# Layer 0 of a two-layer kernel: masks stacked under key parts, three fp16 products in place of f32, another order of work on every engine

## The reference

```python
x = L0_attn_x
xn = layernorm(x)
q, k, v = split(xn @ w_qkv.T)                 # 32, 8 and 8 heads of 64
q, k = rope(rms_norm(q, q_norm_w)), rope(rms_norm(k, k_norm_w))
scores = q @ k.T / 8 + mask                   # -inf outside causal window of 64
attn = softmax(scores) @ v
x = x + attn @ w_out.T + down(silu(gate(xn)) * up(xn))
xn = layernorm(x)
x = x + L1_attn(xn) + L1_ffn(xn)              # L1_attn: LN with ln_w, ln_b; qkv = Xn @ W_in; ...
```

## Time and profile before

| | us |
|---|---|
| median of three runs | 1190.95 |
| the runs | 1176.71 to 1191.04 |
| the profiled execution | 1181.03 |
| its span, first to last instruction | 1179.2 |

### The profile page before, as it was taken

How to read it: one execution, slowest core, us unless ns; L and a number is a source line. 1 busy time by engine, 2 the same in 40 slices (tenths; PEclk the granted TensorE clock), 3 DMA queues, 4 the chain that set the end, 5 groups by cost and what they waited for, 6 DMA issues and landing times. The chain is left out here.

```text
span 1179.2 us, 26751 instructions
## 1 busy us (share of the span) xinstructions
PE 1124.7 (95%) x8985; PEld 676.9 (57%) x8985; DVE 764.1 (65%) x1624; ACT 703.0 (60%) x1703; POOL 709.7 (60%) x1003
## 2 busy tenths in 40 slices
PE   4999999999999999999999999678999999999997
PEld 2677777777777777777777776454333333333324
DVE  5865555656556556556556555447999989887841
ACT  2545445544545445545445444226999999888992
POOL 4777777777777777778778767332455554242221
PEclk9999999999999999999999999879999999999998
DMA  7010100001000000100000000050000000000001
GB/s 277 16 55 22 28 11 21 24 12 26 18 17 22 23 16 21 23 16 22 23 15 22 12 15 18 10 160 1 2 2 3 2 2 2 11 11 11 11 2 36
DMA packets 45801, 30.65 MB, mean 26 GB/s; under 512 B 27684, under 2 KB 44004, under 8 KB 45156
## 3 DMA queue, kind: packets, MB, share of 16 engines
q1 hardware_dynamic: 45668, 28.95, 8.8%
HBM read 18.49 MB, written 4.19 MB: 19 GB/s over the span
## 5 line engine op out<-in xcount | busy, mean ns | idle before, releaser
L1208 DVE TENSOR_REDUCE l_mxv<-l_mx 128x1 f32<-128x1024 f32 x256 | 300.2, 1219 | 39.7 <-PE l_mx L1392 37.2
L1111 ACT ACTIVATE l_prob<-l_sc 128x512 f32<-128x512 f32 x512 | 270.7, 610 | 13.1 <-PE l_sc L1400 12.7
L442 ACT ACTIVATE probs<-sc,neg_bound 128x512 f32<-128x512 f32 x128 | 88.0, 687 | 259.5 <-PE sc L848 259.5
L525 DVE TENSOR_TENSOR t<-qk,tcw 128x320 f32<-128x320 f32 x128 | 62.9, 491 | 248.0 <-ACT v L354 247.1
L649 POOL TENSOR_TENSOR t<-t 128x320 f32<-128x320 f32 x128 | 110.4, 862 | 175.9 <-DVE t L526 175.8
L1392 PE MATMUL l_mx<-l_kt,l_qt 48*128 48x512 f16 x512 | 154.0, 382 | 9.4 <-DVE l_mxv L1208 9.4
L1400 PE MATMUL l_sc<-l_qt,l_kt 50*128 50x512 f16 x512 | 159.4, 382 | 0.9 <-ACT l_prob L1111 0.8
L1372 PE MATMUL l_acc<-l_prob,qkv_all 128*17 128x256 f32 x2048 | 153.9, 384 | 0.0
L640 POOL TENSOR_TENSOR rm<-ss,half_neg 128x5 f32<-128x5 f32 x128 | 152.6, 1192 | 0.0
L807 PE MATMUL pv<-v,probs 128*128 128x65 f32 x1024 | 141.4, 281 | 0.0
L834 PE MATMUL ob<-wo,ats 128*128 128x256 f32 x512 | 131.9, 380 | 0.5 <-ACT ats L354 0.5
(11 more groups left out here) (180 smaller groups left out, 2307.9 us busy)
## 6 DMA issues: line engine op xcount, KB each, us to landing
v<-v SPq DMA_DIRECT2D x240, 16.2 KB, 1.8
qkv_all<-w_qkv SPq DMA_DIRECT2D x3, 768.0 KB, 8.5
xn_all<-xs SPq DMA_DIRECT2D x16, 128.5 KB, 2.0
xa<-x SPq DMA_DIRECT2D x16, 128.0 KB, 2.5
wo<-w_o SPq DMA_DIRECT2D x2, 1024.0 KB, 8.6
xc<-x SPq DMA_DIRECT2D x16, 128.0 KB, 2.3
out<-xc SPq DMA_DIRECT2D x16, 128.0 KB, 2.0
l_wt<-w SPq DMA_DIRECT2D x2, 1024.0 KB, 8.2
```

What stands on the lines that cost most here:

```text
L1111: act.activation(prob[:, (y * NI + u) % NPR, h * 512:(h + 1) * 512], sc[:, k % NSC, :], ACT.Exp, scale=D1 ** -0.5).then_inc(s_["act_sc"], 1)
L1208: dve.tensor_reduce(mxv[:, x % 2, u:u + 1], mx[:, MX[k] % 2, :], AX.X, ALU.max).then_inc(s_["dve_mx"], 1)
```

## The change

**Scores.** The key high part is stored on both halves of the partitions, for a product of full height with `qt` (query low over query high). The low part of the keys stands in the lower half (partitions 64 to 127) of two further stretches of `kts`, with the mask in the upper half, and is multiplied with `qe`, which holds an identity over the query high part. Mask and low part are one product of full height for each window. ScalarE fills in the masks once, in slots 4 and 5. The first two tiles add one more mask product. The second half of S and its wait are gone. The key is turned in two full pieces instead of four half ones.

**Three fp16 products.** `wo` and `win` are loaded into `stage` (four pieces and one, SP waiting for the splits of wq that free the place) and split into high and low fp16 parts, in slots 8 to 15 and 20, 22, 24, on ScalarE and VectorE. The turned context is split too: high part on ScalarE (`ath`), low part on VectorE (`atl`). W is then six fp16 products and the layer-1 projections six each. v is scaled by 8 and the residual sum divides by 512.

**ln_w and ln_b** are applied by ScalarE, as scale and bias of the copy after the turn (Identity); a further copy and a VectorE subtraction split the result. GpSimd's two products are gone.

**Order.** TensorE: gate and up first, A, O, the down projection (a step of its own), V, T, S, W. ScalarE: Tanh and the context's high part ahead of the squares, exp ahead of the key copies. VectorE: context's low part first; sums of squares after the division; query copies last, after the normalisations and the ranking. GpSimd: the table products one a slot over four slots, the rotation over three. The layer-1 projection begins in slot 3 instead of 4 of its tile, and takes one slot more.

```diff
-    return (n + 2) * G + 7 if n >= NT - 2 else (n + 3) * G + 4
+    return (n + 2) * G + 21 - n if n >= NT - 2 else (n + 3) * G + 3
...
+def gated(s):
+    i, r = divmod(s - LAG_F0 - (s < LAG_F0 + 2 * G), 2 * G)
+    return (i, r // 2) if 0 <= i < NI and r % 2 == 0 and r // 2 < NF else (None, None)
...
             # SP
-                if s in (LAG_A + 1, LAG_A + 3):
-                    j = (s - LAG_A) // 2
-                    sp.dma_start(wo[:, j * 4:j * 4 + 4, :, :], w_o[:, j * 4:j * 4 + 4, :, :]).then_inc(wo_ld[j], 16)
+                if s in (LAG_A + 1, LAG_A + 4):
+                    j = 0 if s == LAG_A + 1 else 1
+                    sp.wait_ge(s_["dve_wq"], 6 if j else 3)
+                    for c in range(2 * j, 2 * j + 2):
+                        sp.dma_start(wo_f[c], w_o[:, 2 * c:2 * c + 2, :, :]).then_inc(wo_ld[j], 16)
...
                 if s == 2 * G:
+                    sp.wait_ge(s_["dve_wq"], G)
-                    sp.dma_start(win[:, :, :], w_in).then_inc(l1w_ld, 16)
+                    sp.dma_start(win_f, w_in).then_inc(l1w_ld, 16)
...
             # ScalarE
+                k = s - LAG_W + 1
+                if 0 <= k < G:
+                    act.wait_ge(wo_ld[k // 4], 16 * 2)
+                    ev(wo_hi[:, k, :, :], wo_f[k // 2][:, k % 2, :, :], WS).then_inc(s_["act_w1"], 1)
...
-                    ev(xt1[:, :, :], extra[:, 0:D].rearrange("p (k t) -> p k t", k=KC)).then_inc(s_["act_xat"], 1)
+                    for c in range(KC):
+                        ins = act.activation(xlt[:, c, :], extra[:, c * P:(c + 1) * P], ACT.Identity,
+                                             bias=lnb[:, c:c + 1], scale=lnw[:, c:c + 1])
+                    ins.then_inc(s_["act_xat"], 1)
+                    act.wait_ge(s_["act_xat"], n * 2 + 1)
+                    ev(xt1h[:, :, :], xlt).then_inc(s_["act_xat"], 1)
...
-                    ev(nat[:, b, :, 0:HD], t1[:, b, :, :]).then_inc(s_["act_hi"], 1)
+                    ev(nat[:, b, 0:REP * P].rearrange("p (h d) -> p h d", h=REP)[:, :, HD:P], t1[:, b, 0:REP, :])
+                    ev(nat[:, b, REP * P + HD:NH * P + HD].rearrange("p (a d) -> p a d", a=2),
+                       t1[:, b, REP:NH, :].broadcast_to([P, 2, HD])).then_inc(s_["act_hi"], 1)
...
-                    ev(kts[:, n % B, :, k, 0:WIN], kts[:, n % B, :, k, P:P + WIN]).then_inc(s_["act_kc"], 1)
+                    ev(kts[:, n % B, k, 0:WIN], kts[:, n % B, k, P:P + WIN])
+                    ev(kts[under, n % B, k, near:near + WIN], kts[under, n % B, k, far + WIN:far + P]).then_inc(s_["act_kc"], 1)
+                if s in (LAG_A, LAG_A + 1):
+                    o = far if s > LAG_A else near
+                    act.wait_ge(mk_ld, 16)
+                    ev(kts[upper, :, :, o:o + P].rearrange("p b g c -> p (b g) c"),
+                       mk[upper, 1:2, :].broadcast_to([HD, B * G, P]))
...
-                    ev(kts[:, n % B, :, k, WIN:WIN + P], tr[:, REP:REP + 2, :]).then_inc(s_["act_kt"], 1)
+                    ev(kts[:, n % B, k, WIN:WIN + P], tr[:, REP, :])
+                    ev(kts[under, n % B, k, near + WIN:4 * P].rearrange("p (a c) -> p a c", a=2),
+                       tr[under, REP + 1:REP + 2, :].broadcast_to([HD, 2, P])).then_inc(s_["act_kt"], 1)
...
             # VectorE
+                n, k, ok = at(s, LAG_O)
+                if ok:
+                    dve.wait_ge(s_["act_at"], n * G + k + 1)
+                    wait(dve, s_["pe_W"], n * G + k - 1)
+                    dve.tensor_tensor(atl[:, b, :, :, :].rearrange("p a h q -> p h a q"), atv,
+                                      ath[:, b, :, :, :].rearrange("p a h q -> p h a q"), ALU.subtract).then_inc(s_["dve_al"], 1)
...
+                n = on_way(s, 1)
+                if n is not None:
+                    dve.wait_ge(s_["act_xat"], n * 2 + 2)
+                    dve.tensor_tensor(xt1l[:, :, :], xlt, xt1h[:, :, :], ALU.subtract).then_inc(s_["dve_xt"], 1)
...
+                n, k, ok = at(s, LAG_T)          # now the last block of the loop
+                if ok:
+                    dve.wait_ge(s_["act_kt"], n * G + k + 1)
+                    wait(dve, s_["pe_S"], n * G + k - 1)
+                    dve.tensor_copy(qt[:, b, :, :], tr[:, 0:REP, :])
+                    dve.tensor_copy(qe[under, b, :, :], tr[under, 0:REP, :]).then_inc(s_["dve_qt"], 1)
...
             # TensorE
+                    for j in range(REP + 2):
+                        o = j * P if j < REP else REP * P + HD if j == REP else REP * P - HD
+                        ins = pe.transpose(tr[:, j, :], nat[:, b, o:o + P], idh[:, :])
...
-                        pe.wait_ge(s_["act_at"], t * G + j + 1)
+                        pe.wait_ge(s_["dve_al"], t * G + j + 1)
...
-                    pe.matmul(weights[0], keys(n, k, 1, 0, top), queries(k, 0, top), start=True, stop=False)
-                    pe.matmul(weights[1], outside(n, 1), eyes, start=True, stop=False)
-                    pe.matmul(weights[0], keys(n, k, 0, 0, full), queries(k, 0, full), start=False, stop=False)
-                    pe.matmul(weights[1], keys(n, k, 0, 1, full), queries(k, 1, full), start=False, stop=False
-                              ).then_inc(s_["pe_S1"], 1)
+                    for h in range(2):
+                        ins = pe.matmul(weights[h], fine(n, k, h), queries(qe, k, h), start=True, stop=False)
+                    if n < B:
+                        pe.matmul(weights[0], mk[upper, 0, :], eyes, start=False, stop=False)
+                    for h in range(2):
+                        ins = pe.matmul(weights[h], coarse(n, k, h), queries(qt, k, h), start=False, stop=True)
...
-                        ins = pe.matmul(ob[:, 0:D], ats[:, b, j, :, :], wo[:, k, j, :], start=(k == 0 and j == 0),
-                                        stop=False)
+                        for m, (a, w) in enumerate(((ath, wo_hi), (ath, wo_lo), (atl, wo_hi))):
+                            ins = pe.matmul(ob[:, 0:D], a[:, b, j, :, :], w[:, k, j, :], start=(k == 0 and j == 0 and m == 0),
+                                            stop=(k == G - 1 and j == 1 and m == 2))
...
+                    terms = [(c, a, w) for c in range(KC) for a, w in ((xt1h, win_hi), (xt1h, win_lo), (xt1l, win_hi))]
+                    for m, (c, a, w) in enumerate(terms):
+                        ins = pe.matmul(extra[:, :], a[:, c, :], w[:, c, 0:2 * D], start=(m == 0), stop=(m == len(terms) - 1))
```

More of the change, by code:

```diff
@@ L32 @@
 RMS_EPS, LN_EPS = 1e-6, 1e-5
-WS = 64.0
+WS, VS = 64.0, 8.0
 HID = 704
@@ L594, in _ @@
                     norm_stats(st3, mv3, ve3, xs[:, par, 0:D], par, "dve_b3", "dve_g3", "dve_v3", n)
-                    wait(dve, s_["dve_h"], min(NI * NF, max(0, (s - LAG_F0) // 16 * NF + min(NF, (s - LAG_F0) % 16 // 2 + 1))))
+                    wait(dve, s_["dve_h"], sum(gated(r)[0] is not None for r in range(s + 1)))
                     if n == 0:
@@ L708, in _ @@
[L708 to L712 removed]
+                for r in range(3):
+                    n = on_way(s, 4 if s >= (NT + 1) * G + 2 else 4 + r)
+                    if n is None:
+                        continue
                     heads = qk1_all[:, n % B, n // B, :].rearrange("p (h d) -> p h d", d=D1)[:, :, 0:ROT1]
@@ L854, in _ @@
                     wait(pe, s_["dve_xl"], n)
-                    wait(pe, s_["act_l1"], sum(way(j) + 2 < s for j in range(NT)) * 2)
+                    wait(pe, s_["act_l1"], sum(way(j) + 3 < s for j in range(NT)) * 2)
                     for c in range(KC):
```

345 lines of the change are left out of this document (180 added, 165 removed).

## The result

The changed kernel takes 1105.28 us, median of four runs from 1092.86 to 1113.09; the kernel before, beside it, 1190.99. The ratio is 0.927, interval 0.915 to 0.939: faster. The forecast was 1110 in a range of 1094 to 1142. The profiled execution took 1092.86 us, span 1091.1.

A forecast was written before the change was run, and what follows sets the result against it. TensorE's own work was taken to set layer 0's pace. Span 1179.2 - 89.6 (TensorE) + 10 (waits) + 6 (start) - 1.5 (end) = 1104.1, time 1106, taken as 1110; range 1094 to 1142.

The forecast's parts named there:

- Output projection: TensorE, each slot: six fp16 products at 0.65 us instead of 0.96; gain 0.31 x 128 slots = 39.7 us.
- Scores: TensorE, each slot: four full products, 0.44 us instead of 0.67, a half-height pair counted as two; gain 27.6 us.
- Transposes: TensorE, each slot: six full ones at 0.08, 0.47 us instead of 0.54; gain 9 us.
- Other moves on TensorE change no price: TensorE's group order: moving the gate product ahead of the projection, or down projection ahead of the probabilities, changes no price.
- Layer-1 projections: TensorE, 16 tiles: 1.82 to 1.30 us and 4 x 0.24 to 0.65; gain 0.83 x 16 = 13.3 us.
- Waits: TensorE in layer 0, mainly slot 2's transposes waiting for VectorE's query copies: 1.3 us a repetition, 10 us in all.
- Start: Slots 4 to 15: mask fills and weight splits cost 6 us, bounds 0 and 15; later slot 17 means over 6 wrong.
- End of layer 0 and layer 1: Last tile loses two GpSimd products and its four-pass projection: 1.5 us won; layer 1 as long as before.
- VectorE in lockstep: Rival, layer 0: VectorE's 4.2 us mean hides slots of 5.5, giving 5.3 a slot, time 1140; 17%.
- The loop: Rival: loop through four engines, 8.8 us for two slots, with additions 11.0, 5.5 a slot, about 1155; 8%.
- Port: Rival: VectorE and GpSimd block each other, GpSimd's long products stretch, 5.95 a slot, time 1214, slower; 4%.
- table load: ScalarE's Identity copy priced as a plain copy; own table would cost 2 x 1.28 us per tile, up to 20 us.

The follow-up runs named there:

- a_w32: Changed kernel with the output projection back in fp32, without VectorE's context subtraction and the weight splitting: 1110.21 us, period 79.99.
- a_half: Changed kernel with the scores' two full-height mask/low-key products replaced by one half-height pair, the other halves left out: 1104.89 us, period 79.47.
- b_vt: Kernel before the change, with only the values (probabilities times v) moved ahead of the transposes on TensorE: 1160.97 us, period 87.96.
- a_tv: Changed kernel with the transposes moved back ahead of the values on TensorE: 1139.39 us, period 83.71.
- a_no_wolo: Changed kernel without VectorE's eight splits for the output weight's low part, which stays zero: 1109.02 us, period 78.52.
- a_pad: Changed kernel with the gated layer's last chunk padded from 64 to 128 hidden rows: 1097.63 us, period 78.59.
- a_xl_st: a_xl_early plus the statistics of the second norm put behind the query copies on VectorE: 1088.62 us, period 77.79.
- a_qe_act: Changed kernel with the second query copy on ScalarE, behind the key copies, instead of last on VectorE: 1097.73 us, period 78.23.
- a_best: Changed kernel with three edits: low part of x first on VectorE, second query copy on ScalarE, last chunk padded to 128 rows: 1095.88 us, period 76.74.
- a_xl_early: Changed kernel with the low part of x made first in VectorE's slot instead of behind the norms: 1100.49 us, period 77.77.
- after_same: The changed kernel itself, unedited, run again beside a_best: 1107.35 us, period 78.52.

## Why the prediction was right, point by point

The direction, the bound (TensorE with short waits) and the time, 1110 against 1105, came out. The period of 78.5 instead of 80.5 is two errors of opposite sign, 5.9 us too much work on TensorE and 3.9 too little waiting, so part of the agreement is luck. So is part of the last step: the profiled execution, for which my sum had 1106, took 1092.86, and the median lies higher because of the clock (last section).

- **Output projection, 0.31 a slot.** The price, 0.96 to 0.66, as forecast. Undone alone it gives back 1.46 of the 5.0 us a repetition that I booked (a_w32): 0.10 a slot belonged to the change to the half-height pair behind it, and 1.9 us were eaten by the waits for VectorE, whose subtraction came with it.
- **Scores, 0.23.** The number as forecast, 0.67 to 0.44; my reason was wrong. I read the 0.22 behind a pair as two products and set the rule of products at once aside. Layer 1 shows two halves in the time of one (a_half), and then 0.10 for the change of shape. What the edit took away is the change.
- **Transposes, 0.07.** Wrong: 0.21. I priced six full ones at 0.08 each from the first group of the earlier trace rows. That group lasts 0.31 for four only because the key pieces follow, which use half the columns of the array (128*64 in the row); the pitch is 0.055. a_half shows the same 0.10 with products of half the rows behind them. 0.135 x 128 = 17 us more than the term.
- **"Other moves on TensorE change no price".** The step of the prediction that failed. The values went from 1.04 to 0.84, 0.20 x 128 = 26 us. In the kernel before, the order is worth 0.167 a slot (b_vt); in the new one, with full-height scores behind them, 0.05 (a_tv). So about 0.15 of it is the half-height products on both sides of the values (the key pieces ahead, the pair behind), 0.05 the full-height transposes ahead of them; the edit that moved them and the edit that made the scores and keys full each take most of it alone.
- **Layer-1 projections, 0.83 a tile.** As forecast: 1.82 to 1.30 and 0.96 to 0.65.
- **Waits, 1.3 a repetition.** The place, the releaser and the size of the first one were right: transposes of slot 2, query copy, VectorE's slot 1 of 5.4 us without a pause, 1.5. The size of the whole was not, 5.2. I let TensorE's slot be 3.81 where it is 3.47, so all other hand-offs had 0.35 less slack, and the low part of x, which I costed only as VectorE's time, is what the layer-1 transposes wait for, 0.8. 3.9 x 7.5 = 29 us more than the term.
- Together: 17 + 26 - 29 = 14 us better than the sum, and the span is 1091.1 where I had 1104.1.
- **Start.** My sum had the gain of eight slots and 6 us against it, slot 17 near 84.8; it was 85.17. The sentence that a later slot 17 would mean 6 us of error did not follow from that sum. VectorE's splits of the output weights are the larger part of the 6 (a_no_wolo, 4.0 us).
- **End of layer 0 and layer 1.** -1.5 forecast for the end; the stretch from slot 131 to layer 1 is 4.8 shorter, which includes its share of the cheaper products. Layer 1 is as long as before.
- **Rivals.** VectorE in lockstep was a share of the truth: slots 0 to 3 of the even tile are its, not the mean slot. a_pad and a_xl_st show it: there, time freed on TensorE or order changed on VectorE comes back as a wait. The loop: ScalarE's copy does wait for GpSimd's t (54.7 us in 100 to 600), but no long wait of TensorE ends with it. Moving load to ScalarE (a_qe_act, 83 of 100 in a_best) lengthened VectorE's waits for ScalarE. The terms of my loop add up to 8.5 and not 8.8, so it stood further below the pace than I had it. Port: GpSimd's means of 0.862 and 0.798 are those of before. I looked at GpSimd alone. The low part of x, which I counted among the slowed, reads one operand from PSUM and keeps its 0.413; what gets longer is VectorE's normalisation (last section). No table load came with Identity, but the copy's price was too low: 0.453 for half the columns.

What stays open: how much of the 0.6 a repetition at the scores and of the 0.5 at the other transposes is VectorE's arrears and how much ScalarE's key copies; no run takes one away without the other.

## What to carry to other kernels

Price a TensorE group by the start of the next one, and ask which part of that price belongs to its neighbours: here each change between full and half shapes cost about 0.10 us, so removing the half ones pays in rows that the edit does not touch. An order is a price and a cover at once: before moving a group, look at what waits behind the place it leaves (a_tv: 0.05 of price, 0.28 a slot of waits). When an engine gets near the bound in a few slots, count its work slot by slot; the waits moved on with each single cure, and three cures together (a_best) gave more than their sum.

## What the runs showed of the hardware that I had not expected

**A change of shape on TensorE costs about 0.10 us.** The group ahead of a product that uses fewer rows or columns of the array is longer by 0.10 (transposes ahead of the key pieces or of half-height scores, the output projection ahead of a pair, the values ahead of a pair), and so is the way back (0.21 for a pair of products that run at once, 0.309 against 0.226 in layer 1). The down projection at 64 rows takes 0.62 instead of 0.43, and the values behind it 0.94 instead of 0.84; a_pad takes that away without streaming one column less. Added up over a slot, an estimate from these prices: of the 0.95 us by which the four groups became shorter, about two thirds are changes of shape that are gone; the three fp16 products in place of f32 are 0.21.

**One VectorE instruction waits for GpSimd.** VectorE's normalisation in slot 1 of the changed kernel runs from 323.59 to 324.45 (its row stands with the result). GpSimd's row beside it, the sum of t1 and t2:

```profile
323.44 0.86 POOL L723 TENSOR_TENSOR t<-t 128x320 f32<-128x320 f32 x1
```

It ends 0.15 us after GpSimd's sum. It does so in every kernel here in which it starts within the first 0.6 us of that sum, however late it starts: it takes 0.94 us in the kernel before, 0.86 in the changed one, 0.70 in a_half, 0.53 in a_qe_act and a_xl_early, 0.43 in a_best. In a_w32 and a_tv it starts in the last 0.15 us of the sum, ends 0.15 after GpSimd's next instruction and takes 1.05 and 1.01. In slot 0, where it never starts beside that sum, it takes 0.41. So up to 0.6 us of the slot that TensorE waits for depends on where GpSimd stands, and each edit moves that as well.

**The scatter is time at the lower clock.** Windows between the layers and near the end, the changed kernel first, then a_no_wolo:

```profile
680.00:690.00 10.00, 3.87 (x19) 3.90 (x19) 1.05 (x5) 0.00 (x0) 5.63 (x16) 0.50 0.88 261
...
700.00:710.00 10.00, 9.05 (x64) 4.68 (x64) 8.29 (x7) 1.85 (x4) 1.45 (x6) 1.00 0.00 0
...
1080.00:1090.00 10.00, 8.42 (x35) 4.83 (x33) 2.12 (x5) 1.24 (x4) 0.00 (x0) 1.00 0.22 74
```

```profile
700.00:710.00 10.00, 10.00 (x36) 3.01 (x33) 4.92 (x5) 1.25 (x3) 0.00 (x0) 0.50 0.00 0
...
1080.00:1090.00 10.00, 10.00 (x25) 5.67 (x24) 1.27 (x3) 1.15 (x3) 0.00 (x0) 0.50 0.12 39
```

Between the layers TensorE is busy 4 to 5 of 10 us and the granted clock falls to 0.50, that is 1.2 GHz. In the first run it is back at 1.00 (2.4 GHz) by 700, in the second not before 710, though TensorE is no less busy there. The same again at the end: from 1080 us on the first run has 1.00, the second 0.50 to its last instruction, with TensorE busy 10.00 of 10. In that run the part behind GpSimd's first fill is 432.8 us long instead of 412.8, with the same code: about 9 us are lost in the first 60 us of it and about 11 in the last 35, and in between the two run alike. Up to the fill, from slot 131 on, both take 36.9. The six runs of after_same go with the mean granted clock in the same way: 1093.5 us at 0.975, 1104.9 at 0.965, 1110.6 at 0.962. That is a spread of 1.5% which no edit of layer 0's repetitions made, and the reason to judge such edits by the starts of slots, which agree within 0.2 us between two runs of the same kernel (641.44 and 641.61).
